# Six token tiles instead of four through all experts densely, in an adaLN layer with capacity-routed experts on one Trainium2 core

## The reference

```python
h = layernorm(x) * (1 + ca) + sa
x = x + ga * attn(h)              # linear attention with 8 heads, its MLP, two layer norms
h = layernorm(x) * (1 + cb) + sb
# the expert layer, xt = h as 4096 tokens
probs = softmax(xt @ Wg)                          # [4096, 8]
_, top_idx = top_k(probs.T, cap)                  # each expert takes its 512 best tokens
sel[e, top_idx[e]] = True
assigned = sel.any(axis=0)
tok2exp = where(assigned, argmax(where(sel, probs.T, -inf), axis=0), argmax(probs.T, axis=0))
weights = probs[token, tok2exp[token]]
for e in range(E):
    gate = where(tok2exp == e, weights, 0.0)
    out += gate[:, None] * (gelu(xt @ W1[e]) @ W2[e])
x = x + gb * out
```

## Time and profile before

| | |
|---|---|
| median of 3 runs | 232.55 us (232.32 to 233.91) |
| the profiled execution | 233.0 us, of which the span from first to last instruction is 231.3 us |
| busy | TensorE 181.5 us (78%), VectorE 168.3 (73%), GpSimd 151.9 (66%), ScalarE 131.9 (57%) |
| mean granted TensorE clock | 0.876 of full speed |

### The profile page before, as it was taken

How to read it: one execution, slowest core, us unless ns; L and a number is a source line. 1 busy time by engine, 2 the same in 40 slices (tenths; PEclk the granted TensorE clock), 3 DMA queues, 4 the chain that set the end, 5 groups by cost and what they waited for, 6 DMA issues and landing times.

```text
span 231.3 us, 4246 instructions
## 1 busy us (share of the span) xinstructions
PE 181.5 (78%) x1161; PEld 142.8 (62%) x1161; DVE 168.3 (73%) x565; ACT 131.9 (57%) x425; POOL 151.9 (66%) x236
## 2 busy tenths in 40 slices
PE   0879989999799999966585879977589989998000
PEld 0636867978578988865325366545388879997000
DVE  1769789699997899897988879899006998654100
ACT  2149984366646889963986862342516767764000
POOL 8797838358564666664699960047777777777771
PEclk9999999999979999985557556999979999999855
DMA  5996000000010000000066223003333333111110
GB/s 164 272 273 202 0 3 1 3 0 0 7 41 0 1 4 0 0 3 0 15 203 202 83 83 98 4 23 91 92 112 106 101 96 113 48 58 48 57 45 23
DMA packets 16966, 15.48 MB, mean 67 GB/s; under 512 B 1904, under 2 KB 14320, under 8 KB 16944
## 3 DMA queue, kind: packets, MB, share of 16 engines
q1 hardware_dynamic: 14288, 9.70, 14.2%
q0 software_dynamic: 2240, 5.51, 7.8%
q10 hardware_dynamic: 416, 0.01, 0.1%
HBM read 8.92 MB, written 6.29 MB: 66 GB/s over the span
## 4 chain that ended last, share of the span: by engine, by line
PE 48%; DVE 26%; ACT 8%; POOL 7%; issue 6%; DMA 2%; POOLq 0%; DVEq 0%; ACTq 0%
PE pH L986 6%; DVE scr L1322 6%; POOL out_dram L434 6%; PE pQ L995 6%; PE pQ L893 5%; PE pH L816 4%; PE pQ L827 3%; DVE t L1144 3%; PE pH L883 2%; DVE x_sb L1200 2%; PE pQ L808 2%; DVE x_sb L1146 2%; DMA x_sb<-in_L_attn_x_dram 2%; PE pT L836 2%; PE pG L733 2%
## 5 line engine op out<-in xcount | busy, mean ns | idle before, releaser
L431 POOL DMA_INDIRECT rows<-table_dram,gidx x28 | 28.9, 1030 | 24.5 <-DVE gidx L1414 16.3
L434 POOL DMA_INDIRECT out_dram<-rows,gidx x28 | 27.4, 980 | 8.5 <-issue 6.1
L986 PE MATMUL pH<-x_sb,hid 128*128 (+1 forms) x140 | 22.6, 284 | 1.1 <-ACT hid L649 1.0
L995 PE MATMUL pQ<-ew,u 128*128 (+1 forms) x140 | 22.3, 282 | 1.2 <-ACT u L663 0.7
L995 PEld LDWEIGHTS pQ<-ew,u 128*128 128x128 f32 x140 | 18.4, 191 | 3.0 <-issue 1.6
L663 ACT ACTIVATE u<-pH 128x256 f32<-128x256 f32 x35 | 13.4, 383 | 11.5 <-PE pH L986 11.4
L986 PEld LDWEIGHTS pH<-x_sb,hid 128*128 128x128 f32 x140 | 18.4, 191 | 2.2 <-issue 1.8
L1463 DVE SCALAR_TENSOR_TENSOR t<-pQ,wslot,scr 128x128 f32<-128x128 f32 x35 | 12.1, 344 | 10.2 <-PE pQ L995 9.6
L536 ACT ACTIVATE sqj<-pQ 128x128 bf16<-128x128 f32 x60 | 15.8, 283 | 6.0 <-PE pQ L827 3.0
L299 POOL TENSOR_TENSOR yr<-yv,neghalf 128x4 f32<-128x4 f32 x16 | 17.0, 1064 | 1.3
L299 POOL TENSOR_TENSOR rs<-ve,neghalf 128x4 f32<-128x4 f32 x16 | 16.3, 1018 | 1.3
(11 more groups left out here) (330 smaller groups left out, 533.1 us busy)
## 6 DMA issues: line engine op xcount, KB each, us to landing
table_dram<-x_sb SPq DMA_DIRECT2D x9, 256.0 KB, 2.8
x_sb<-in_L_attn_x_dram SPq DMA_DIRECT2D x8, 256.0 KB, 5.3
table_dram<-rows SPq DMA_DIRECT2D x7, 256.0 KB, 2.4
ew<-in_L_ffn_W_dram SPq DMA_DIRECT2D x2, 512.0 KB, 9.0
w1d<-in_L_ffn_W_dram SPq DMA_DIRECT2D x1, 1024.0 KB, 11.2
rows<-table_dram,gidx POOLq DMA_INDIRECT x28, 2.7
out_dram<-rows,gidx POOLq DMA_INDIRECT x28
wmod_sb<-in_L_wmod_dram SPq DMA_DIRECT2D x1, 384.0 KB, 4.9
```

The lines of the kernel that those rows point to most:

```text
L431: gp.indirect_dma_start(row[:, t, :], None, table[:, :], bass.IndirectOffsetOnAxis(gidx[:, t:t + 1], 0)).then_inc(gathered[t], 16)
L434: gp.indirect_dma_start(out.rearrange("b l d -> (b l) d"), bass.IndirectOffsetOnAxis(gidx[:, t:t + 1], 0), row[:, t, D:2 * D], None).then_ ...
L986: mm = te.matmul(pH[i % 2][:, f * P:(f + 1) * P], wcur[:, i % RW, f * P:(f + 1) * P], xt[:, bass.ds(i - e, 1), :], start=True, stop=True)
L995: mm = te.matmul(pQ[i % 2][:, 0:D], eh[:, i % 2, f * P:(f + 1) * P], ew[:, bass.ds(e, 1), f * D:(f + 1) * D], start=(f == 0), stop=(f == 1))
```

## The change

Six tiles (`ND`) take the dense way, so `NP` falls from 28 to 26 and `NI` from 35 to 33. `TRUE` maps the order of processing to the order in memory: the two last groups of memory, which hold the dense tiles, are processed fifth and sixth (`DH` = 4, half of it dense; `DG` = 5, all of it), and the two other groups of the second sequence seventh and eighth. Their normalisation moves to ScalarE (`ROWS_ON_ACT`), group 3's to the place behind the loop. The transposes for the dense part move from behind the search's preparation to the last front stage, ahead of `p_tx3(7)`.

In the search a round may hold two ups or a whole down; twelve ups and four downs stand there instead of five and two. A few matmuls of no use (`busy`) stand before and in round 0. Downs 5 and 7 get a second bank, `pL`, and downs from 5 on wait for the copy but one. The two further tiles have steps of their own (`h_up`, `h_gelu`, `h_down`, `half_step`), behind the 16 ups and 8 downs, and the items wait for them.

```diff
+ND = 6
+NP = NT - ND
+NI = NP + E - 1
+TRUE = (0, 1, 2, 3, 6, 7, 4, 5)
+DG = 5
+DH = 4
+DW = (ND - GT) * P
+ROWS_ON_ACT = (0, 1, 2, DH, DG, 3)
-QUARTERS = (4, 4, 3, 3)
+QUARTERS = (4, 3, 3, 3)
+HALVES = (7, 6)
+RUNS = (((0, 0, TB),), ((TB // 2, 0, TB // 2), (0, TB // 2, TB // 2)))
...
+        def down_bank(e):
+            return pL if e >= GT and e % 2 else pQ0
+        def half_bank(e):
+            return (pH1, pT, pQ0, pG)[e // 2][:, e % 2 * DW:(e % 2 + 1) * DW]
...
-            sp.wait_ge(S["out_d"], 1)
-            sp.dma_start(out.rearrange("b (p t) d -> b p t d", p=P)[B - 1, :, TB - GT:TB, :], bgroup(x_sb, DG))\
+            sp.wait_ge(S["out_d"], 2)
+            sp.dma_start(out.rearrange("b (p t) d -> b p t d", p=P)[B - 1, :, TB - ND:TB, :], x_sb[:, NP:NT, :])\
...
             # ScalarE, last front loop
-                if 0 <= s - 6 < ACT_ROWS:
+                if 6 <= s <= 8:
                     a_xn3(s - 6)
                 if 0 <= s - 3 < G - 1:
                     a_square(s - 3, 1, "y2_ready", "sq2")
+                if s == G + 1:
+                    a_xn3(DH)
+                if s == G + 3:
+                    a_xn3(DG)
+            a_h2_dense(0)
             a_soft(1)
-            a_xn3(G - 1, range(0, 2))
+            a_xn3(3, range(0, 2))
             a_soft(2)
-            a_xn3(G - 1, range(2, GT))
+            a_xn3(3, range(2, GT))
...
-            between = {0: (a_h2_last,), 1: (d_gelu, 0), 2: (d_gelu, 1), 3: (d_gelu, 2), 5: (d_copy, 0), 6: (d_gelu, 3), 7: (d_gelu, 4),
-                       9: (d_copy, 1)}
+            between = {0: ((a_h2_dense, 1), (d_gelu, 0)), 1: ((d_gelu, 1), (d_gelu, 2)), 2: ((d_copy, 0),), 3: ((d_gelu, 3), (d_gelu, 4)),
+                       4: ((d_gelu, 5),), 5: ((d_copy, 1),), 6: ((d_gelu, 6), (d_gelu, 7)), 7: ((d_copy, 2),),
+                       8: ((d_gelu, 8), (d_gelu, 9)), 9: ((d_copy, 3),)}
...
             # TensorE
             def p_tx_dense():
-                te.wait_ge(S["xn3"], ACT_ROWS + 1)
+                te.wait_ge(S["relu0"], G)
+                te.wait_ge(S["xn3"], ROWS_ON_ACT.index(DG) + 1)
+                for t in range(ND - GT):
+                    te.transpose(txd_bank(1)[:, t * P:(t + 1) * P], xn[:, DH, 2 * GT - ND + t, :], ident[:, :])
                 for t in range(GT):
...
                 if 0 <= s - 5 < G and s > G:
                     p_lg(s - 5)
+                if s == G + 3:
+                    p_tx_dense()
                 if 0 <= s - 4 < G:
                     p_tx3(s - 4)
...
+            def h_up(e):
+                te.wait_ge(S["gelu_d"], 2 * E + e - 2)
+                if e == 0:
+                    te.wait_ge(S["h2_last"], 2)
+                for f in range(2):
+                    mm = te.matmul(up_bank(2 * E + e)[:, f * DW:(f + 1) * DW], w1d[:, e, f * P:(f + 1) * P], h2d[1], start=True, stop=True,
+                                   skip_group_check=True)
+                mm.then_inc(S["up_d"], 1)
+            def h_down(e):
+                te.wait_ge(S["gelu_d"], 2 * E + e + 1)
...
+                for t in range(ND - GT):
+                    for f in range(2):
+                        mm = te.matmul(half_bank(e)[:, t * D:(t + 1) * D], ehd[e % 2][:, f, t * P:(t + 1) * P], ew[:, e, f * D:(f + 1) * D],
+                                       start=(f == 0), stop=(f == 1), skip_group_check=True)
+                mm.then_inc(S["down_d"], 1)
...
-                        te.wait_ge(S["copy_d"], e)
+                        te.wait_ge(S["copy_d"], e - 1 if e > GT else e)
...
+            def busy(k):
+                for _ in range(k):
+                    te.matmul(pF[:, 0:B * P], onesb[:, :], segmask[:, :], start=True, stop=True, skip_group_check=True)
             p_prt(0)
-            between = ((d_up, 0), (d_up, 1), (d_up, 2), (d_down_half, 0, 0), (d_down_half, 0, 1), (d_up, 3), (d_up, 4), (d_down_half, 1, 0),
-                       (d_down_half, 1, 1))
+            d_up(0)
             p_prt(1)
-            p_tx_dense()
+            d_up(1)
+            busy(2)
+            between = (((busy, 2), (d_up, 2)), ((d_down, 0),), ((d_up, 3), (d_up, 4)), ((d_up, 5),), ((d_down, 1),),
+                       ((d_up, 6), (d_up, 7)), ((d_down, 2),), ((d_up, 8), (d_up, 9)), ((d_down, 3),), ((d_up, 10), (d_up, 11)))
...
-            d_down(4)
-            d_up(11)
-            d_down(5)
-            d_up(12)
-            d_up(13)
             d_down(6)
-            d_up(14)
-            d_up(15)
+            h_up(0)
             d_down(7)
+            h_up(1)
+            for e in range(2, 5):
+                h_up(e)
+                h_down(e - 2)
...
+            p_weights(0)
+            p_weights(1)
+            for e in range(5, E):
+                h_up(e)
+                h_down(e - 2)
+            h_down(E - 2)
+            h_down(E - 1)
+            te.wait_ge(S["acc_h"], 6)
             p_xt(0)
...
             # VectorE
-                dve.tensor_tensor(pr[:, b, :, :], pe_[:, b, :, :], sm[:, b, :].unsqueeze(1).to_broadcast([P, E, TB]),
-                                  ALU.mult).then_inc(S["probs"], 1)
+                for run in RUNS[b]:
+                    to, ts, n = run
+                    last = dve.tensor_tensor(pr[:, b, :, to:to + n], pe_[:, b, :, ts:ts + n],
+                                             sm[:, b, ts:ts + n].unsqueeze(1).to_broadcast([P, E, n]), ALU.mult)
+                last.then_inc(S["probs"], 1)
...
+            def half_step(e):
+                dve.wait_ge(S["down_d"], E + (e | 1) + 1)
+                y = half_bank(e).rearrange("p (t d) -> p t d", d=D)
+                if e == 0:
+                    dve.tensor_copy(acch[:, :, :], y).then_inc(S["acc_h"], 1)
+                else:
+                    dve.wait_ge(S["acc_h"], e)
+                    dve.copy_predicated(acch[:, :, :], wd[:, 0:ND - GT, e:e + 1].bitcast(I32).to_broadcast([P, ND - GT, D]), y)\
+                       .then_inc(S["acc_h"], 1)
...
             for t in range(AHEAD):
                 gate(t)
+            for e in range(2):
+                half_step(e)
             dve.wait_ge(S["inv_ready"], 3)
...
+            for e in range(2, E):
+                half_step(e)
```

More of the change, by code:

```diff
@@ L38 @@
 FIRST = 14
-ACT_ROWS = 5
-NP = NT - GT
+TRUE = (0, 1, 2, 3, 6, 7, 4, 5)
[3 more added lines that the diff above has]
+ROWS_ON_ACT = (0, 1, 2, DH, DG, 3)
+KEPT = tuple(g for g in range(G) if g != DG)
 NB = NP // 2
-QUARTERS = (4, 4, 3, 3)
-DG = G - 1
+QUARTERS = (4, 3, 3, 3)
+HALVES = (7, 6)
 SOFT = ((0, slice(0, TB)), (1, slice(0, TB - GT)), (1, slice(TB - GT, TB)))
 SOFT_GROUPS = (GB, G - 1, G)
+RUNS = (((0, 0, TB),), ((TB // 2, 0, TB // 2), (0, TB // 2, TB // 2)))
 SHARED = 2
@@ L217, in bgroup, with xgroup, xtile, tiles_of @@
             return t[:, g * GT:(g + 1) * GT, :]
+        def xgroup(g):
+            return bgroup(x_sb, TRUE[g])
+        def xtile(g, t):
+            return x_sb[:, TRUE[g] * GT + t, :]
+        def tiles_of(g):
+            t0 = TRUE[g] % GB * GT
+            return slice(t0, t0 + GT)
         def lg_out(g):
@@ L422, in _ @@
             gp.wait_ge(S["keys"], 1)
-            for g in range(DG):
-                h2tok(g)
+            for k, g in enumerate(KEPT):
+                h2tok(k, g)
             gp.wait_ge(S["tab_done"], 16 * 2 * G)
@@ L619, in _ @@
                     act.copy(klo_ps, ki[:, 1, :]).then_inc(S["klo_ready"], 1)
-                if n in between:
-                    step, *what = between[n]
-                    step(*what)
+                for step, what in between[n]:
+                    step(what)
             act.wait_ge(S["over_ready"], 1)
@@ L640, in _ @@
             d_gelu(15)
+            d_copy(6)
+            h_gelu(0)
+            d_copy(7)
+            h_gelu(1)
+            h_gelu(2)
+            h_gelu(3)
             held = []
@@ L653, in _ @@
                 a_weights(i)
-            d_copy(6)
-            d_copy(7)
+            for e in range(4, E):
+                h_gelu(e)
             def a_xt(t):
@@ L921, in _ @@
                           skip_group_check=True).then_inc(S["totals"], 1)
-                if n < len(between):
-                    step, *what = between[n]
-                    step(*what)
+                for step, what in between[n]:
+                    step(what)
             te.matmul(pL[:, 0:B * E], onesb[:, :], shift[:, 0, :], start=True, stop=False, skip_group_check=True)
@@ L928, in _ @@
               .then_inc(S["thr_ready"], 1)
-            d_up(5)
+            d_up(12)
             te.wait_ge(S["sover_ready"], 1)
@@ L936, in _ @@
                       skip_group_check=True).then_inc(S["base_ready"], 1)
-            d_up(6)
-            d_down(2)
-            d_up(7)
+            d_down(4)
+            d_up(13)
             te.matmul(pT[:, 0:B * E], onesb[:, :], shift[:, 1, :], start=True, stop=False, skip_group_check=True)
@@ L948, in _ @@
                       skip_group_check=True).then_inc(S["rbase_ready"], 1)
-            d_up(8)
```

(24 more changed lines are left out.)

120 lines of the change are left out of this document (61 added, 59 removed).

## The result

The changed kernel takes 230.76 us (median of 14 runs, 229.56 to 231.68) against 232.77 for the kernel before in the same sessions (14 runs, 230.82 to 234.24). The ratio is 0.9916, 95% interval 0.9890 to 0.9942: 0.8% faster, 2.0 us. The forecast was 231.2, 1.3 us faster. The profiled execution took 229.56, its span is 227.6, which is the fast end of its runs. In this and all later comparisons the medians take in every run, and the ratios leave out the runs more than 1.5% above the fastest of the same kernel.

What follows compares the result with a forecast made beforehand. The bound was GpSimd's gapless issue of 56 indirect DMAs and how late `gidx` starts it. Savings of 5.2 and 0.2 us against costs in front and search summed to -1.3, from 232.55 to 231.2 us; range 228.6 to 235.5.

Steps and rivals of the forecast that it cites:

- Two gathers and two scatters fewer: GpSimd's queue: two gathers at 1.33 us and two scatters at 1.29 us fall away, 5.2 us off.
- Slack of the item stage: Item 7's sum ready at 34.7 us after `gidx`, scatter 0 free at 35.7: slack 1.0 us, cost 0.
- Half steps beside the gathers: VectorE's eight half steps beside GpSimd's gathers: cost 0, at worst 3.2 us through the shared port.
- Front: Last front stages: late normalisation and dense transposes delay `p_tx3(7)` by 1.7 us; second probabilities in two pieces add 0.1.
- Search: Search rounds: down waiting for its gelu 0.2 us, low clock in round 1 or 2 1.0, fall around round 3 0.5.
- Two ups in round 9: End of the search: two ups delay the matmul that VectorE waits for by 0.6 us (2.7 at low clock).
- Selection: Selection ahead of `gidx`: one-hots for two fewer tiles save 0.2 us on VectorE's chain.
- rival 1: Front and clock cost nothing: -3.9 us, 228.6 us; its sign a `gidx` no later than 153.5; chance 0.17.
- (2): Clock stays low in the search, each double round costing 1.5 us: 234.3 to some 242, middle 237; chance 0.14.
- (3): Dense part beside the gathers becomes the bound, scatter 0 waits 4 of 5 extra us: 234.6 us; chance 0.10.
- (4): GpSimd's gathers held up by VectorE's half steps, 3.2 us: 234.4 us; chance 0.04 given for this and 5.
- 5: The number of indirect DMAs does not set the kernel's end; no size given; chance 0.04 given for this and (4).

Runs made afterwards that it cites:

- g1: The kernel before with its last two scatters left out (two output tiles unwritten): 230.07 us, ratio 0.9867 to the kernel before.
- d3: The changed kernel with 28 matmuls of no use ahead of the first item: 230.87 us, ratio 0.9931 to the kernel before.
- d8: The changed kernel with 75 matmuls of no use ahead of the first item: 236.01 us, ratio 1.0085 to the kernel before.
- a_again: The changed kernel measured once more, no edit: 230.48 us, ratio 0.9908 to the kernel before.
- f1: The changed kernel with ScalarE's normalisation of group 4 one stage later and one more scratch tile: 229.05 us, ratio 0.9841 to the kernel before.
- f2: The changed kernel with TensorE's dense transposes behind `p_tx3(7)`, not ahead of it: 229.14 us, ratio 0.9853 to the kernel before.
- c1: The changed kernel with the edits of f1, f2 and s1 together: 226.65 us, ratio 0.9756 to the kernel before.
- s1: The changed kernel with round 9's two ups behind the threshold-bits matmul and `d_up(12)` behind the sums for `sel`: 230.31 us, ratio 0.9889 to the kernel before.
- s2: The changed kernel without the matmuls of no use before and in round 0: 230.88 us, ratio 0.9929 to the kernel before.

## Why the prediction was right

The sum was -1.3 and the result is -2.0. The mechanism was the forecast one: GpSimd's queue gets shorter by four DMAs, and about 3 us are given back ahead of its first entry. That the sum came within 0.7 us is in part luck, since the terms for the clock are means over falls that came in some profiles and not in others. The terms:

- **Two gathers and two scatters fewer, -5.2.** Measured 2.36 + 2.48 = 4.8. I took the mean distance of all gathers, 1.33, where the two that fall away cost 1.18 each, nearer to the short ones of 1.25. g1 confirms the mechanism and the price of a scatter.
- **Slack of the item stage, 1.0.** It was 3.8 between the rows (item 7's sum at 186.0, scatter 0 at 189.81), and 2.8 in time by d3 and d8. Item 0 came 21.4 after `gidx` and not 23.5. As forecast, the dense rest left no pause (TensorE busy 12.00 of 12.0 us between 160 and 172 at a clock of 1.00); it was the price of the steps that was too high, 19 us from the inversion to the last half down and not 21. A half up took 0.87 and a half down 0.89, for which I had 0.95 and 1.0.
- **Half steps beside the gathers, 0.** Right: the gather at 170.53 took 0.94 while VectorE's `copy_predicated` of the half steps ran from 170.80. (The row that I gave for it in the kernel before, 179.76, meets the end of the `copy_predicated` at 179.08 only by 0.05 us; the gather beside it is the one at 178.50, which took 0.95 as well.) What the Trainium skill, page "SBUF — State Buffer", section "Who interferes with whom", allows at worst did not happen here.
- **Front, +1.7 and +0.1.** Measured 1.5 and 1.8, counted from x1(5) to the search. Both parts were as described, the wait for `nm` (1.17 on ScalarE) and the transposes ahead of `p_tx3(7)`. x1(7) comes 9.15 and 9.14 after x1(5), in the kernel before 8.56: later by 0.6, as I had it. (Counted from x1(6) it is 1.2, but x1(6) itself comes 0.57 earlier.) In a_again `p_tx3(7)` is at 12.95 from x1(5), where I had 12.88. f1 and f2 each take one away, c1 both.
- **Search, +0.2 and +1.0 and +0.5.** Measured 1.3 and 0.3 in the two profiles of the changed kernel, 1.4 to 1.5 in s1, s2, d3 and d8, 0 in f1, f2 and c1. So the 1.7 together was too much for each of them. There are two events. The low clock in the first down (3.60 to 3.79 us) is the 1.3 to 1.5. The fall around round 3, for which I had 0.5, came in one profile, a_again, and cost 0.3; in f1 the clock stayed at 1.00 through the same pause of 1.38 us. The 0.2 for a down that waits for its gelu is the wait of 0.17 ahead of L958 at 116.39, and it costs nothing where the clock is high: the search then takes 25.86, as before.
- **Two ups in round 9, +0.6.** Measured 0.57 against the profile of before (0.84) and 0.76 against g1 (0.64); s1 takes it away.
- **Selection, -0.2.** Measured -0.36.
- **Left out.** The last DMAs land 0.3 to 0.4 us sooner after the last scatter; the sum had no term for it.
- **Signs.** `gidx` came at 153.70 and 154.84, 1.5 and 2.6 later than before and not 4, close to the sign of rival 1 (153.5) in the first profile, which had the fast front. The second probabilities were transposed at 110.60 and 112.78 (112.4 forecast), the granted clock rose around 120 in the first (0.54 from 116 to 119, 0.89 to 122, then 1.00; 118 forecast), `eq` waited 1.19 and 1.18, and the DMAs took 68 us, without gaps.
- **Rivals.** The clock was low for one down of the search and not for all of it (2), the dense part is about 3 us from being the bound (3), GpSimd is not held up by the half steps (4), and g1 speaks against 5. Rival 1 had the price of a free front and search, -3.9, and c1 goes beyond it: with the front's and the bits' losses taken out and a gain of 0.57 ahead of x1(6), the same six dense tiles are worth 2.4%, 5.7 us.

## What to carry to other kernels

When the end is a queue that issues without a pause, shorten the queue, and then look at what delays its first entry: here nearly 5 us were gained at the end and about 3 given back ahead of it, most of it not because TensorE had more to do, but because steps were put ahead of the step that the chain waited for. A moved step has to be followed on each engine with the question who makes its input, and in which stage: three edits of order without any change of the work brought more than the change itself. Where a clock falls at a different place in each execution, compare a trace with one in which it fell at the same place: against a_again f2 seemed worth 0.6 us, against s1, whose clock was the same up to that step, 1.04, with which the single moves add up to the combined one within 0.2 us. And count a stage from the last row that the change cannot have moved, here x1(5) and not x1(6).
